# Sixteen exponentials per score tile with a summed output, inverses turned beside the probabilities, and a new setup and order

## The reference

```python
x = x + L0_xattn(layernorm(x), ctx, ctx, fside, mask)     # 16 heads of width 8, 77 keys
x = x + L0_ffn(layernorm(x))                              # 8 experts, top 2 by one-hot slots, capacity 64, F = 512
x = x + L1_xattn(layernorm(x), ctx, ctx, ..., attn_mask = fside_SxS2)
x = x + L1_ffn(layernorm(x))                              # 8 experts of 128x128, top 2 of 10, every expert computed
# attention, per head:
scores = q k^T / sqrt(8) + bias ; scores = where(mask == 0, -1e9, scores)
out = softmax(scores) v ; return concat(out) Wo^T + bo
```

## Time and profile before

| | |
|---|---|
| time, median of 3 runs | 414.07 us (413.9 to 415.3) |
| profiled execution | 414.41 us, span 412.6 us |
| mean granted TensorE clock | 0.937 |
| PE, PEld busy | 335.0, 250.1 us |
| DVE busy | 267.6 us |
| ACT busy | 172.1 us |
| POOL busy | 188.9 us |

### The profile page before, as it was taken

How to read it: one execution, slowest core, us unless ns; L and a number is a source line. 1 busy time by engine, 2 the same in 40 slices (tenths; PEclk the granted TensorE clock), 3 DMA queues, 4 the chain that set the end, 5 groups by cost and what they waited for, 6 DMA issues and landing times.

```text
span 412.6 us, 8817 instructions
## 1 busy us (share of the span) xinstructions
PE 335.0 (81%) x3625; PEld 250.1 (61%) x3633; DVE 267.6 (65%) x629; ACT 172.1 (42%) x317; POOL 188.9 (46%) x211
## 2 busy tenths in 40 slices
PE   3985597587899999999999989999776886787382
PEld 2982366265679777788778867886634553454120
DVE  0132558849666855766766766775898889877632
ACT  3000323132736546374646636563623443353222
POOL 9202534364737334646536443520763376254214
PEclk9999996959999999999999999999995999699867
DMA  3996314130504022000000000000000000000000
GB/s 98 251 366 207 93 39 132 32 101 0 132 2 132 4 54 79 0 3 2 0 3 1 3 2 2 2 2 0 4 1 25 2 2 1 27 2 0 27 1 25
DMA packets 26363, 19.15 MB, mean 46 GB/s; under 512 B 1909, under 2 KB 24275, under 8 KB 26323
## 3 DMA queue, kind: packets, MB, share of 16 engines
q1 hardware_dynamic: 26163, 18.56, 15.4%
q0 software_dynamic: 160, 0.02, 0.3%
HBM read 17.53 MB, written 1.05 MB: 45 GB/s over the span
## 4 chain that ended last, share of the span: by engine, by line
PE 60%; DVE 21%; ACT 9%; issue 4%; POOL 3%; SPq 1%; DMA 1%; POOLq 0%; DVEq 0%; ACTq 0%
PE PB L809 10%; PE HBK L891 8%; PE EBK L906 7%; DVE SC L1228 7%; PE SP L790 6%; ACT PT L533 5%; PE SP L771 4%; PE HBK L914 4%; DVE mx L1230 3%; DVE rc L1236 3%; PE HBK L956 2%; PE SP L775 2%; PE MB L748 2%; PE EBK L956 2%; PE PB L815 1%
## 5 line engine op out<-in xcount | busy, mean ns | idle before, releaser
L351 POOL TENSOR_TENSOR SC<-SC,mx 128x1232 f32<-128x1232 f32 x32 | 72.0, 2250 | 136.9 <-DVE mx L1230 136.8
L533 ACT COPY PT<-SP 128x512 f32<-128x512 f32 (+1 forms) x96 | 44.4, 521 | 41.0 <-PE SP L790 41.0
L790 PE MATMUL SP<-ident,SC 128*128 128x128 f32 x320 | 48.1, 298 | 12.3 <-ACT SC L525 6.4
L790 PEld LDWEIGHTS SP<-ident,SC 128*128 128x128 f32 x320 | 40.4, 154 | 21.8 <-issue 12.5
L525 ACT ACTIVATE SC<-SC 128x1232 f32<-128x1232 f32 x32 | 39.3, 1229 | 33.5 <-POOL SC L351 33.4
L1230 DVE TENSOR_REDUCE mx<-SC 128x16 f32<-128x1232 f32 x32 | 46.0, 1436 | 1.1
L1236 DVE RECIPROCAL rc<-PB 128x128 f32<-128x128 f32 x32 | 30.5, 952 | 16.5 <-PE PB L809 16.5
L809 PE MATMUL PB<-PT,VB 128*32 128x128 f32 x768 | 30.8, 299 | 12.5 <-ACT PT L533 11.7
L891 PE MATMUL HBK<-ein,wi_s 128*128 128x128 f32 x256 | 36.8, 287 | 2.6 <-ACT hT L551 2.6
L891 PEld LDWEIGHTS HBK<-ein,wi_s 128*128 128x128 f32 x256 | 31.0, 191 | 10.9 <-ACT hT L551 5.5
L551 ACT ACTIVATE hT<-HBK 128x512 f32<-128x512 f32 x32 | 19.1, 597 | 41.1 <-PE HBK L891 41.0
(11 more groups left out here) (174 smaller groups left out, 577.1 us busy)
## 6 DMA issues: line engine op xcount, KB each, us to landing
BI<-in_fside_Bx16xSxS SPq DMA_DIRECT2D x8, 1232.0 KB, 6.3
wi_s<-in_L_ffn_wi SPq DMA_DIRECT2D x1, 2048.0 KB, 10.8
X<-in_x SPq DMA_DIRECT2D x4, 256.0 KB, 3.6
out<-acc SPq DMA_DIRECT2D x4, 256.0 KB, 2.1
MI<-in_mask_BxSxS_ik SPq DMA_DIRECT2D x8, 77.0 KB, 7.0
ew_s<-in_L_ffn_expert_w SPq DMA_DIRECT2D x1, 512.0 KB, 4.9
ctxn<-in_ctx SPq DMA_DIRECT2D x1, 154.0 KB
am<-in_fside_SxS SPq DMA_DIRECT2D x1, 154.0 KB, 2.5
```

The lines of the kernel that those rows point to most:

```text
L351: g.tensor_tensor(S4, S4, m4, ALU.subtract).then_inc(s["shifted"], 1)
L533: sc.copy(PT[:, c0:c1, :].rearrange("p c t -> p (c t)"), SP[:, n, 0:(c1 - c0) * P]).then_inc(s["PTs"], 1)
L790: last = te.transpose(SP[:, n, (c - c0) * P:(c - c0 + 1) * P], SC[i % 2][:, c * P:(c + 1) * P], ident[:])
```

## The change

Scores are now written negated (-(scores) - bias), and the minimum per head takes the maximum's place, so that ACT computes exp(-SC + mx) with the minimum as the bias operand. ACT does this per head, sixteen instructions of 77 columns per tile, each with a summed output sm[:, h]; POOL's subtraction is gone. Three of the sixteen release PE's three parts of turns. DVE takes the reciprocal of the sixteen sums (`invert`), POOL spreads it to 128 columns (`spread`), PE turns that as an eleventh block behind the last part, and it arrives in PT's last column block; `normalise` is one product, and `weigh_values` does no sums. The copy of PT waits for the product instead of for the weighing.

In the setup X is loaded first, masks before biases, and the weights in three groups; DVE does most memsets; `values(0)` to `values(3)`, the second layer's keys and the output biases are spread over attention runs 0 and 1. The order is no longer made of stretches but written out piece by piece for each engine. Several pieces get a wait of their own for buffers that the order had kept apart (f_xTcopy, gelu, scale_q, a_xTr, f_xTr). The removed `stretch` functions and most of the new lists are cut from the diff below.

```diff
-        PT = sb("PT", [P, NC, P])
-        rc = sb("rc", [P, P])
+        sm = [sb(f"sm{n}", [P, H]) for n in range(2)]
+        si = [sb(f"si{n}", [P, H]) for n in range(2)]
+        sr = [sb(f"sr{n}", [P, H, DK]) for n in range(2)]
+        PT = sb("PT", [P, NC + 1, P])
...
 @block.sync
+            load_x(0, "ld_x0")
             sp.dma_start(ctxn[:], ctx_in.rearrange("b j d -> j b d")).then_inc(s["ld_ctx"], 16)
+            load_w(0, 1, "ld_wa")
+            load_w(0, 0, "ld_wa")
+            load_col(0, 1, "ld_ca")
+            load_col(0, 0, "ld_ca")
+            load_mask(0, 0)
+            load_bias(0, 0)
+            load_w(0, 2, "ld_wb")
+            load_w(0, 3, "ld_wb")
+            load_w(1, 2, "ld_wb")
...
 @block.gpsimd
-            def shift(a, i):
-                pool.wait_ge(s["rowmax"], NT * a + i + 1)
-                S4 = heads_of(SC[i % 2])
-                m4 = mx[i % 2][:].rearrange("p (u h) -> p u h", u=2).unsqueeze(3).broadcast_to([P, 2, H // 2, J])
-                g.tensor_tensor(S4, S4, m4, ALU.subtract).then_inc(s["shifted"], 1)
+            def spread(a, i):
+                t = NT * a + i
+                pool.wait_ge(s["invd"], t + 1)
+                if t >= 2:
+                    pool.wait_ge(s["trE"], 3 * (t - 1))
+                g.tensor_copy(sr[i % 2][:], si[i % 2][:].unsqueeze(2).broadcast_to([P, H, DK])).then_inc(s["spreadd"], 1)
...
+            block_rows()
+            identity()
+            a_rstd(0)
+            identity_bf16()
+            head_rows()
+            mask_out(0, 0)
+            block_keys(0, 0, "k_kb")
+            spread(0, 0)
...
 @block.scalar
             def softmax_exp(a, i):
-                act.wait_ge(s["shifted"], NT * a + i + 1)
-                S3 = halves_of(SC[i % 2])
-                sc.activation(S3, S3, ACT.Exp).then_inc(s["probs"], 1)
+                t = NT * a + i
+                act.wait_ge(s["rowmax"], t + 1)
+                if t >= 2:
+                    act.wait_ge(s["invd"], t - 1)
+                S4, n = heads_of(SC[i % 2]), i % 2
+                for h in range(H):
+                    Sh = S4[:, h // (H // 2), h % (H // 2), :]
+                    ins = sc.activation(Sh, Sh, ACT.Exp, bias=mx[n][:, h:h + 1], scale=-1.0,
+                                        accum_out=sm[n][:, h:h + 1])
+                    if h in LAST:
+                        ins.then_inc(s["probs"], 1)
...
             def gelu(f, e):
                 act.wait_ge(s["m_h"], NE * f + e + 1)
+                if f > 0 or e >= 4:
+                    act.wait_ge(s["m_eo"], NE // 2 * f + (e - 4) // 2 + 1)
...
+            gelu(1, 3)
+            softmax_exp(3, 0)
+            copy_eo(1, 0)
+            f_xTcopy(2)
+            gelu(1, 4)
+            copy_eo(1, 1)
+            gelu(1, 5)
+            route_exp("m_route", ROUTE0, 2, "m_exp", NE, 2)
+            copy_PT(3, 0, 0)
+            copy_PT(3, 0, 1)
+            copy_eo(1, 2)
+            softmax_exp(3, 1)
+            gelu(1, 6)
...
 @block.tensor
             def turn_probs(a, i, n, c0, c1):
                 t = NT * a + i
+                pe.wait_ge(s["probs"], 3 * t + n + 1)
...
+                if n == 2:
+                    pe.wait_ge(s["spreadd"], t + 1)
+                    last = te.transpose(SP[:, n, (c1 - c0) * P:(c1 - c0 + 1) * P],
+                                        sr[i % 2][:].rearrange("p h d -> p (h d)"), ident[:])
...
             def weigh_values(a, i):
-                for m in range(2):
-                    for n, ks in enumerate(ROUNDS):
-                        for k in ks:
-                            q, c = BLOCKS[k]
-                            mine = [j for j in range(NB) if BLOCKS[j][0] == q]
-                            w = VB[:, a, k, :] if m == 0 else rowmask[:, k].rearrange("p h d -> p (h d)")
-                            last = te.matmul(PB[32 * q:32 * (q + 1), m * P:(m + 1) * P], w, PT[:, c, :],
-                                             start=(k == mine[0]), stop=(k == mine[-1]))
+                for n, ks in enumerate(ROUNDS):
+                    for k in ks:
+                        q, c = BLOCKS[k]
+                        mine = [j for j in range(NB) if BLOCKS[j][0] == q]
+                        last = te.matmul(PB[32 * q:32 * (q + 1), 0:P], VB[:, a, k, :], PT[:, c, :],
+                                         start=(k == mine[0]), stop=(k == mine[-1]))
...
+            turn_ctx()
+            turn_weights((0, 1), "ld_wa", 0)
+            a_xTr(0)
+            keys(0)
+            query(0, 0)
+            attn_scores(0, 0, 0)
+            turn_weights((2, 3, 6), "ld_wb", 1)
+            attn_scores(0, 1, 0)
+            values(0)
+            turn(0, 0, 0)
...
+            project(7, 3, 1)
+            experts(6, 2)
+            experts(6, 3)
+            f_xTr(7)
...
 @block.vector
+            def fill():
+                for t, x in ((half[:], -0.5), (identb[:], 0.0), (rowmask[:], 1.0), (incl[:], 1.0), (strict[:], 1.0),
+                             (ones[:], 1.0), (SC[0][:].rearrange("p (u x) -> p u x", u=2)[:, :, HJ // 2:], 0.0),
+                             (SC[1][:].rearrange("p (u x) -> p u x", u=2)[:, :, HJ // 2:], 0.0), (eb_s[:], 0.0)):
+                    v.memset(t, x).then_inc(s["c_dset"], 1)
...
-                v.tensor_tensor(o, i0, i1, ALU.add).then_inc(s["added"], 1)
+                v.scalar_tensor_tensor(o, i0, -1.0, i1, ALU.mult, ALU.subtract).then_inc(s["added"], 1)
                 dve.wait_ge(s["added"], t + 1)
-                v.tensor_reduce(mx[i % 2][:].rearrange("p (u h) -> p u h", u=2), heads_of(S_), AX.X, ALU.max)\
+                v.tensor_reduce(mx[i % 2][:].rearrange("p (u h) -> p u h", u=2), heads_of(S_), AX.X, ALU.min)\
                     .then_inc(s["rowmax"], 1)
+
+            def invert(a, i):
+                t = NT * a + i
+                dve.wait_ge(s["probs"], 3 * t + 3)
+                if t >= 2:
+                    dve.wait_ge(s["spreadd"], t - 1)
+                v.reciprocal(si[i % 2][:], sm[i % 2][:]).then_inc(s["invd"], 1)
 
             def normalise(a, i):
                 t = NT * a + i
                 dve.wait_ge(s["pv"], t + 1)
-                v.reciprocal(rc[:], PB[:, P:2 * P]).then_inc(s["recips"], 1)
-                dve.wait_ge(s["recips"], t + 1)
-                v.tensor_tensor(oT[:], PB[:, 0:P], rc[:], ALU.mult).then_inc(s["normed"], 1)
+                v.tensor_tensor(oT[:], PB[:, 0:P], PT[:, NC, :], ALU.mult).then_inc(s["normed"], 1)
```

More of the change, by code:

```diff
@@ L489, in _ @@
[L489 to L492 removed]
+            block_rows()
[6 more added lines that the diff above has]
+            spread(0, 0)
+            mask_out(0, 1)
+            spread(0, 1)
+            a_rstd(1)
@@ new lines, in _ @@
+            project(1, 1, 0)
+            a_xTr(2)
+            dispatch(0, 1)
+            weigh_values(1, 2)
+            turn_C(0, 0)
+            query(2, 0)
+            turn(1, 3, 0)
+            project(1, 2, 0)
+            turn_C(0, 1)
+            turn_C(0, 2)
+            turn(1, 3, 1)
+            turn_C(0, 3)
+            attn_scores(2, 0, 0)
+            up(0, 0)
+            weigh_values(1, 3)
+            attn_scores(2, 1, 0)
+            up(0, 1)
+            up(0, 2)
+            down(0, 0)
@@ new lines, in _ @@
+            turn(3, 3, 0)
+            turn_C(2, 2)
+            project(3, 2, 0)
+            turn_C(2, 3)
+            turn(3, 3, 1)
+            up(2, 0)
+            weigh_values(3, 3)
+            query(4, 1)
+            project(3, 3, 0)
+            up(2, 1)
+            attn_scores(4, 0, 1)
+            up(2, 2)
+            down(2, 0)
+            up(2, 3)
+            up(2, 4)
+            up(2, 5)
+            up(2, 6)
+            attn_scores(4, 1, 1)
+            down(2, 1)
+            f_xTr(3)
@@ new lines, in _ @@
+            turn(4, 2, 1)
+            project(4, 1, 1)
+            weigh_values(4, 2)
+            dispatch(3, 1)
+            turn_C(3, 0)
+            turn(4, 3, 0)
+            turn_C(3, 1)
+            turn_C(3, 2)
+            query(5, 1)
+            turn_C(3, 3)
+            turn(4, 3, 1)
+            project(4, 2, 1)
+            up(3, 0)
+            attn_scores(5, 0, 1)
+            up(3, 1)
+            attn_scores(5, 1, 1)
+            up(3, 2)
+            down(3, 0)
+            up(3, 3)
@@ new lines, in _ @@
+            expert_bias(4)
+            attn_scores(5, 3, 1)
+            weigh_values(5, 1)
+            experts(4, 0)
+            turn(5, 2, 0)
+            a_xTr(6)
+            project(5, 1, 1)
+            turn(5, 2, 1)
+            experts(4, 1)
+            weigh_values(5, 2)
+            experts(4, 2)
+            turn(5, 3, 0)
+            project(5, 2, 1)
+            turn(5, 3, 1)
+            query(6, 1)
+            weigh_values(5, 3)
+            project(5, 3, 1)
+            attn_scores(6, 0, 1)
@@ new lines, in _ @@
+            a_xTr(7)
+            turn(6, 2, 1)
+            weigh_values(6, 2)
+            turn(6, 3, 0)
```

(15 more changed lines are left out.)

1614 lines of the change are left out of this document (974 added, 640 removed).

## The result

Median 471.81 us (467.5 to 475.99, 4 runs) against 413.99 us (413.46 to 415.3, 4 runs) of the kernel before in the same rounds: ratio 1.1357, 95% interval 1.1271 to 1.1442. The change costs 57 us; 384 was forecast, and the range ended at 404. The profiled execution took 470.91 us, span 469.2, mean granted clock 0.85 (before 0.937).

The account below looks back on a forecast made before the run. PE was taken to bound most first-layer stretches, DVE to be fullest in second-layer ones, and a tile's chain to set those with gaps. Stage terms, -22 from setup, summed to -30.4 from 414.41: 384 us, range 366 to 404.

Parts of the forecast that it names:

- Part 1: Setup: statistics no longer behind the value matmuls; first add at 16.3 us, gain 25 us, net -22 us.
- rival (c): Setup: PE's first long stretch keeps slow matmuls or value weights land late; 10 to 15 us more, 394 to 399; chance 0.10.
- Parts 2 and 3: Weighing and normalising: denominators leave PE (3.0 to 3.5 us per stretch), wide reciprocals leave DVE (3.0 us per stretch).
- Part 4: Softmax on ACT: sixteen exponentials with sums take 5.7 us a tile, adding 17.9 us per stretch of four tiles.
- low end: Exponentials on ACT if the sum is free: 0.210 us per added head, 3.4 to 3.5 us a tile.
- Part 5: Tile chain and new waits: loses about 5.1 us, gains 5.7 of exponentials; where order doesn't hide it, 2 us a stretch.
- the sum: Whole kernel: stage-by-stage changes together -30.4 us against 414.41, giving 384 us.
- (d): ACT's queue: gelus wait behind a tile's exponentials and PE's up() behind them; +12 us, 396; chance 0.10.
- (b): ACT becomes the bound everywhere: 441 us at 8.1 us a tile, sign turning at 7.0; chance 0.11.
- (e): New order removes more latency than credited, ACT at 5.7 us a tile: 376 us; chance 0.12.
- (a): Exponentials' sum nearly free, 3.5 to 4.6 us a tile, PE stays the bound: 369 us; chance 0.20.

Follow-up runs that it names:

- e15: Changed kernel, setup and order kept, with one row minimum as bias of one wide exponential and PE denominators, no POOL subtraction: 413.59 us, ratio 1.0075 to the kernel before.
- e9: Changed kernel's setup with the stretch order and softmax of the kernel before: 404.73 us, ratio 0.9776 to the kernel before.
- e12: Changed kernel's setup with the order of before, one row minimum as bias of one wide exponential, PE denominators, no POOL subtraction: 399.96 us, ratio 0.9748.
- e2: Changed kernel with four wide exponentials per tile in place of sixteen, without bias and sums: 391.5 us, ratio 0.9438 to the kernel before.
- e1: Changed kernel with only the summed output of its exponentials left out, sums being constants: 408.06 us.
- e3: Kernel before, its setup and order kept, with the new softmax alone: 505.15 us, ratio 1.2177 to the kernel before.

## Why the prediction was wrong

**Part 1, the setup: right in the first add, and by luck in the sum.** The first add came at 13.28 (16.3 forecast, 41.46 before), with X's statistics at 3.41. S and A together ended at 51.63, 21.2 us earlier for a forecast of 22, but two terms that the forecast had not are in that: with cheap exponentials the new order ends A at 43.4 (e15), and the price of the exponentials took 8 us of it back. With order and softmax of before the setup gave 12.8 us by the end of A, and 9 in all. There rival (c) is what came: "PE's first long stretch stays at its slow matmuls", A 13.9 us longer than before (10 to 15 said), and only some 5 of the 14 us more of PE there are the work that was moved (e9 against e12).

**Parts 2 and 3: right in size, and their worth not seen in the changed kernel.** The weighing has 768 records instead of 1536. The reciprocal took 0.25 us (0.2 taken), the spread copy 0.29 (0.45), the add 1.44 as before (+0.06 taken). DVE ended at 234; "near 250" was said, though eight stretches at 3.8 us less come to 237. With cheap exponentials these parts may be worth up to 22 us (e2 against e15, a reading only).

**Part 4, the exponentials: right in size.** 5.5 us a tile for 5.7 taken, ACT 315 for some 322, the two extra table loads there too (1.28 us each, 0.1 to 0.2 us of idle ahead of eight or nine). The low end was too low: sixteen exponentials without a sum take 4.10 us, so 0.25 a head and not the 0.210 that I scaled from 128 columns. The Trainium skill (ScalarE: Activation LUTs, What ACT_TABLE_LOAD costs) has figures from which 251 ns follow (an estimate: 280 ns + 0.833 for each of 77 columns, less 93 of overlap), and the run without sums agrees.

**Part 5 and the sum: the step that failed.** "C, D, E: the fullest engine goes from PE 44.4 to ACT 44.6; with the 2.3 us of idle that PE had, 47." ACT was at 45.1 and 48.5 in C and D (44.6 forecast), and the stages were 62 and 64. The errors by stage, against the sum's own terms: S and A +1, B +6.5, C +15, D +17, E +10, F +17, G +6, H +13.5, T +1, in all 87 of the 87 us. (The sum's +1 for E is a slip: a stage of 47 there is +2.3.) The 2.3 us was not a property of the stage but of one order with one engine full: PE's idle in D was 2.3 us in the old order with ACT at 26, 5.0 in the new order with ACT at 31 (e15), 8.4 with ACT at 42.5 (e1), 13.8 with ACT at 48.5. Two engines with 45 and 42 us of work that hand it to each other all along a stage need not fit into 47: each gelu, each copy of PT and each copy of expert output (W) sits behind a block of up to 5.5 us. So the step that failed is the overlap: it was taken as complete but for 2.3 us, and PE was idle 11.1, 13.8, 11.2 and 13.4 us in C, D, E and F. I also carried PE's durations over at the granted clock of 1.00; as PE waited more, the clock fell to 0.87 to 0.92 in C to F, and PE's 42.0 became 50.7, of which some 3 us were there at a clock of 1.00 too (e1, 45.4 in D).

**The rivals.** (d) named the mechanism, gelus and with them `up` behind a tile of exponentials, and its sign (PE and ACT both idle in a stage over 50), at 50 to 51 us for C to F; it was 56 to 64, because it counted two gelus of 2 us where copies of PT and of expert output are held as well, and left the clock out. (b) put the turn of the sign at 7.0 us a tile, by ACT becoming full; without ACT ever being full it came at about 4.1 (408.1 us at 4.0, 42 us per us above). (e), that the new order removes latency, fell: it costs 13.6 us (e15 against e12). (a) assumed that a free sum leaves 369; the run without sums is 408, 39 us above it, so a free sum would not have made that rival true.

**What the 57 us are.** Setup -9 (e9); one bias a row in place of the POOL pass -5 (e12, not clear of noise); the new order +14 (e15); inverses turned beside the probabilities and turns released in parts -22 (e2); sixteen exponentials with a bias each in place of four +17 (e1); their sums +63. These steps depend on each other, and some compare runs of different rounds: in the old order and setup the new softmax cost 91 us (e3). What share of the last 63 the lower clock would cost by itself stays open: PE's account puts up to 33 us on it, and no run held the clock without adding work. Nor was a kernel tried that joins A and B of the new order (10 us better) to the old order behind them.

## What to carry to other kernels

Before work is moved to an engine that is less than full, ask what stands behind it in that engine's queue and who waits for it: here 128 us of work that nobody needed, given to an engine 44 to 48% busy, cost 75 and 76 us in the two orders. A stage's length is not that of its fullest engine plus an old remainder once two engines that feed each other are both near it; take the remainder from a stage with both loads, or put a block of the new length into the queue and measure. Split a change into setup, order and operation, each alone: here the setup was a gain, the order and the summed exponentials were losses, and the gain could be had without them. And compare a stage's busy time only at the same granted clock: 9 us that looked like moved work in e9 were the same records, slower.
